# Query and key stacks: one transfer of 48 partitions per half instead of three of 16, the high part stored twice in DRAM

## The reference, cut to what matters

```
q = split_heads(query @ Wq.T + bq)      # 16 heads of 16 features
k = split_heads(key @ Wk.T + bk)
scores = einsum('bhqd,bhkd->bhqk', q, k) / sqrt(16)
scores = where(mask == 0, -1e9, scores)
x = softmax(scores) @ v
```

## Time and profile before

| | |
|---|---|
| runs | 1540.78 us median (1537.13 to 1541.7) |
| the profiled execution | 1551.78 us |
| its span | 1550.0 us |
| granted TensorE clock, mean over the span | 0.915 |
| TensorE matmul busy | 1268.1 us, 82% |
| VectorE busy | 1097.4 us, 71% |
| ScalarE busy | 958.6 us, 62% |
| GpSimd busy | 691.8 us, 45% |
| `ks<-ksplit_d` transfers | 192 of 128 KB |
| `qs<-qsplit_d` transfers | 192 of 128 KB |

### The profile page before, as it was taken

How to read it: one execution, slowest core, us unless ns; L and a number is a source line. 1 busy time by engine, 2 the same in 40 slices (tenths; PEclk the granted TensorE clock), 3 DMA queues, 4 the chain that set the end, 5 groups by cost and what they waited for, 6 DMA issues and landing times.

```text
span 1550.0 us, 29933 instructions
## 1 busy us (share of the span) xinstructions
PE 1268.1 (82%) x9486; PEld 878.3 (57%) x9486; DVE 1097.4 (71%) x3076; ACT 958.6 (62%) x1846; POOL 691.8 (45%) x854
## 2 busy tenths in 40 slices
PE   4962365688899989998999899989998999888875
PEld 4851354456566656665666566656665666555543
DVE  4753342458788878887888788878886777777754
ACT  1220231257777767776777777767766777777774
POOL 2312334235544554456445644565446444444331
PEclk9985586699999989998999999999998999999996
DMA  8772354445445445554544455545444444333200
GB/s 273 228 255 56 99 178 146 142 145 157 142 149 155 152 139 150 152 158 134 151 150 150 151 153 148 154 141 150 142 140 127 132 145 126 120 104 103 76 9 14
DMA packets 169174, 216.84 MB, mean 140 GB/s; under 512 B 19002, under 2 KB 157628, under 8 KB 162492
## 3 DMA queue, kind: packets, MB, share of 16 engines
q1 hardware_dynamic: 162876, 198.15, 41.8%
q0 software_dynamic: 6144, 16.79, 3.2%
HBM read 133.33 MB, written 79.43 MB: 137 GB/s over the span
## 4 chain that ended last, share of the span: by engine, by line
PE 47%; DVE 22%; issue 14%; ACT 5%; DMA 4%; POOL 4%; SPq 3%; DVEq 0%; another core or an unknown queue 0%; POOLq 0%; ACTq 0%
DVE mx L1104 8%; PE mx_pair L1369 5%; PE bank L1330 5%; PE ex_pair L1314 4%; PE bank L1442 4%; PE bank L1340 4%; PE bank L1396 3%; PE mx_pair L1292 3%; PE bank L1390 3%; DVE small L1160 3%; PE mx_pair L1356 3%; PE bank L1450 2%; PE bank L1410 2%; DVE t L1155 2%; DVE bn L899 2%
## 5 line engine op out<-in xcount | busy, mean ns | idle before, releaser
L1104 DVE TENSOR_REDUCE mx<-mx_pair 128x4 f32<-128x1024 f32 x256 | 312.7, 1222 | 60.0 <-PE mx_pair L1369 36.2
L694 POOL TENSOR_TENSOR hid<-hid,t 128x256 f32<-128x256 f32 x256 | 196.3, 771 | 227.4 <-DVE t L1155 226.0
L846 ACT ACTIVATE pt<-ex_pair 128x1024 f32<-128x1024 f32 x256 | 262.1, 1024 | 26.0 <-PE ex_pair L1314 25.8
L1369 PE MATMUL mx_pair<-ks,qs 62*128 62x256 f32 x1024 | 133.3, 336 | 67.8 <-DVE mx L1104 57.8
L1330 PE MATMUL bank<-pt,va 128*32 128x256 f32 x2048 | 169.7, 404 | 2.0 <-ACT ot L852 1.9
L1369 PEld LDWEIGHTS mx_pair<-ks,qs 62*128 62x128 f32 x1024 | 85.6, 196 | 144.0 <-DVE mx L1104 120.1
L871 ACT ACTIVATE hid<-bank 128x256 f32<-128x256 f32 x256 | 98.6, 385 | 109.0 <-PE bank L1340 100.3
L1314 PE MATMUL ex_pair<-qs,ks 64*128 64x256 f32 x1024 | 132.5, 338 | 7.8 <-ACT pt L846 7.7
L1442 PE MATMUL bank<-ew,xst 128*128 x480 | 125.5, 406 | 6.4 <-ACT xst L815 6.2
L1155 DVE SCALAR_TENSOR_TENSOR t<-th,bank 128x256 f32<-128x256 f32 x256 | 106.8, 417 | 33.5 <-ACT th L877 21.2
L661 POOL TENSOR_TENSOR rs<-ve,mhalf 128x2 f32<-128x2 f32 x96 | 68.6, 714 | 132.1 <-DVE ve L905 112.0
(11 more groups left out here) (212 smaller groups left out, 2757.4 us busy)
## 6 DMA issues: line engine op xcount, KB each, us to landing
ks<-ksplit_d SPq DMA_DIRECT2D x192, 128.0 KB
qs<-qsplit_d SPq DMA_DIRECT2D x192, 128.0 KB, 3.1
ys_d<-ys SPq DMA_DIRECT2D x56, 256.0 KB, 2.2
xs<-xs_d SPq DMA_DIRECT2D x24, 512.0 KB
x<-in_x SPq DMA_DIRECT2D x32, 256.0 KB, 3.9
va<-in_ctxT SPq DMA_DIRECT2D x32, 256.0 KB, 3.6
xl<-in_x SPq DMA_DIRECT2D x32, 256.0 KB
x_d<-xl SPq DMA_DIRECT2D x32, 256.0 KB, 3.7
```

Of the source, the lines that this page charges most:

```text
L694: pool.tensor_tensor(part_, part_, t1[:, c % 2], ALU.mult).then_inc(hid_made, 1)
L846: act.activation(pt[:, slot:slot + 2].rearrange("p i a c -> p (i a c)"), ex_pair[:, :], ACT.Exp).then_inc(ex_made[u % 2], 1)
L1104: dve.tensor_reduce(mx[:, t].rearrange("p (r g j) -> p r g j", r=2, j=2)[:, :, g], mx_pair[:, :].rearrange("p (r j s) -> p r j s", r=2, j= ...
L1369: ins = pe.matmul(shared_bank(job, r)[:, j * S:(j + 1) * S], qs[par][rows, 2 * g + j, t * P:(t + 1) * P], ks[par][rows, 2 * g + j, :], sta ...
```

## The change

The DRAM scratch holds three parts of each tensor instead of two, in the order in which the stack wants them. The high part is written twice. A half of a stack is then 48 consecutive partitions, and is filled by one transfer. The counts on the semaphores follow: 48 instead of 32 for written parts, 64 instead of 128 for the k stack, 32 instead of 96 for the q stack. The same number of bytes is read.

```
-        ksplit_d = scratch("ksplit_d", [2, 2, D, S])
-        qsplit_d = scratch("qsplit_d", [2, 2, D, S])
+        ksplit_d = scratch("ksplit_d", [2, ROWS, D, S])
+        qsplit_d = scratch("qsplit_d", [2, ROWS, D, S])
...
                 if job == "k_write":
-                    for i, src in enumerate((ph, pl)):
+                    for i, src in enumerate((ph, ph, pl)):
                         sp.dma_start(ksplit_d[b.par, i].rearrange("(k p) s -> p k s", p=P), src[:].bitcast(F32)).then_inc(k_wr[b.par], 16)
                 if job == "k_read":
-                    landed(sp, k_wr, b, 32)
+                    landed(sp, k_wr, b, 16 * ROWS)
...
-                    for row, i in ((0, 0), (1, 0), (2, 1)):
-                        for r in range(2):
-                            sp.dma_start(ks[b.par][r * HALF + row:r * HALF + row + ROWS * (DH - 1) + 1:ROWS].bitcast(F32),
-                                         ksplit_d[b.par, i].rearrange("(d r h) s -> r d h s", d=DH, r=2)[r]).then_inc(ks_ld[b.par], 16)
+                    for r in range(2):
+                        sp.dma_start(ks[b.par][r * HALF:r * HALF + ROWS * DH].bitcast(F32),
+                                     ksplit_d[b.par].rearrange("c (d r h) s -> r d c h s", d=DH, r=2)[r]).then_inc(ks_ld[b.par], 16)
...
                 if job == "q_write":
-                    for i, src in enumerate((ph, pl)):
+                    for i, src in enumerate((ph, pl, ph)):
                         sp.dma_start(qsplit_d[b.par, i].rearrange("(k p) s -> p k s", p=P), src[:].bitcast(F32)).then_inc(q_wr[b.par], 16)
                 if job == "q_read":
-                    landed(sp, q_wr, b, 32)
+                    landed(sp, q_wr, b, 16 * ROWS)
...
-                    for row, i in ((0, 0), (1, 1), (2, 0)):
-                        for r in range(2):
-                            sp.dma_start(qs[b.par][r * HALF + row:r * HALF + row + ROWS * (DH - 1) + 1:ROWS].bitcast(F32),
-                                         qsplit_d[b.par, i].rearrange("(d r h) s -> r d h s", d=DH, r=2)[r]).then_inc(qs_ld[b.par], 16)
+                    for r in range(2):
+                        sp.dma_start(qs[b.par][r * HALF:r * HALF + ROWS * DH].bitcast(F32),
+                                     qsplit_d[b.par].rearrange("c (d r h) s -> r d c h s", d=DH, r=2)[r]).then_inc(qs_ld[b.par], 16)
```

More of the change, by code:

```diff
@@ L557, in work @@
                     after(sp, kl_made, b)
-                    landed(sp, ks_ld, b.ago(2), 128)
-                    for i, src in enumerate((ph, pl)):
+                    landed(sp, ks_ld, b.ago(2), 64)
+                    for i, src in enumerate((ph, ph, pl)):
                         sp.dma_start(ksplit_d[b.par, i].rearrange("(k p) s -> p k s", p=P), src[:].bitcast(F32)).then_inc(k_wr[b.par], 16)
                 if job == "k_read":
-                    landed(sp, k_wr, b, 32)
+                    landed(sp, k_wr, b, 16 * ROWS)
                     after4(sp, sc_ready[1], b.ago(2), 4)
@@ L575, in work @@
                     after(sp, ql_made, b)
-                    landed(sp, qs_ld, b.ago(2), 96)
-                    for i, src in enumerate((ph, pl)):
+                    landed(sp, qs_ld, b.ago(2), 32)
+                    for i, src in enumerate((ph, pl, ph)):
                         sp.dma_start(qsplit_d[b.par, i].rearrange("(k p) s -> p k s", p=P), src[:].bitcast(F32)).then_inc(q_wr[b.par], 16)
                 if job == "q_read":
-                    landed(sp, q_wr, b, 32)
+                    landed(sp, q_wr, b, 16 * ROWS)
                     after4(sp, sc_ready[1], b.ago(2), 4)
-                    for row, i in ((0, 0), (1, 1), (2, 0)):
-                        for r in range(2):
-                            sp.dma_start(qs[b.par][r * HALF + row:r * HALF + row + ROWS * (DH - 1) + 1:ROWS].bitcast(F32),
-                                         qsplit_d[b.par, i].rearrange("(d r h) s -> r d h s", d=DH, r=2)[r]).then_inc(qs_ld[b.par], 16)
+                    for r in range(2):
+                        sp.dma_start(qs[b.par][r * HALF:r * HALF + ROWS * DH].bitcast(F32),
+                                     qsplit_d[b.par].rearrange("c (d r h) s -> r d c h s", d=DH, r=2)[r]).then_inc(qs_ld[b.par], 16)
                 if job == "max_row":
@@ L699, in work @@
                     after(pool, m01_made, b)
-                    landed(pool, ks_ld, b.ago(2), 128)
+                    landed(pool, ks_ld, b.ago(2), 64)
                     pool.tensor_scalar(mbias[:, b.par], mk[96:98, b.par], 0, nbig[96:98, 0:1], ALU.is_equal, ALU.mult).then_inc(mb_made, 1)
@@ L705, in work @@
                     after(pool, kf_made, b)
-                    landed(pool, q_wr, last_q(b), 32)
+                    landed(pool, q_wr, last_q(b), 16 * ROWS)
                     pool.tensor_tensor(pl[:], pf[:], ph[:].bitcast(F32), ALU.subtract).then_inc(kl_made, 1)
@@ L717, in work @@
                     after(pool, qh_made, b)
-                    landed(pool, k_wr, last_k(b), 32)
+                    landed(pool, k_wr, last_k(b), 16 * ROWS)
                     pool.tensor_tensor(pl[:], pf[:], ph[:].bitcast(F32), ALU.subtract).then_inc(ql_made, 1)
@@ L818, in work @@
                     after(act, kf_made, b)
-                    landed(act, q_wr, last_q(b), 32)
+                    landed(act, q_wr, last_q(b), 16 * ROWS)
                     act.activation(ph[:], pf[:], ACT.Copy).then_inc(kh_made, 1)
@@ L827, in work @@
                     after(act, kl_made, last_k(b))
-                    landed(act, k_wr, last_k(b), 32)
+                    landed(act, k_wr, last_k(b), 16 * ROWS)
                     for dst in (pf, ph):
@@ L1361, in work @@
                     if c == 0:
-                        landed(pe, qs_ld, b, 96)
-                        landed(pe, ks_ld, b, 128)
+                        landed(pe, qs_ld, b, 32)
+                        landed(pe, ks_ld, b, 64)
                     for r in range(2):
```

## The result

The changed kernel takes 1559.38 us (median of four runs, 1554.78 to 1563.3), the kernel before 1541.24 on the same chip (four runs, 1537.13 to 1542.77). The ratio is 1.0112, with a 95% interval of 1.0082 to 1.0142: the change costs 1.1%, about 17 us. 1540 had been predicted, in a range that ended at 1552. The profiled execution took 1563.3 us, with a span of 1561.5 against 1550.0; since the profiled execution of before lay above its timed runs, the two traces are 11.5 us apart where the timed runs are 17 to 18.

What follows compares the result with a forecast made beforehand. TensorE was taken as the bound (busy 82%, 47% of the chain), with SP's issue time mattering only on q's path. For q, +0.8 - 0.8 - 0.3 = -0.3 us, all else 0, gave 1 us less: 1540 us, range 1534 to 1552.

Steps and rivals of the forecast that it cites:

- (a): Third write of q: its transfer queues on the DMA engines and delays q's stack by 0.8 us, bounds +0.47 to +0.9.
- (b): Two reads of the q stack instead of six: first issue to completion 5.4 us instead of 6.2, a shift of -0.8.
- D: In (b), time for 0.79 MB to flow, 2.75 us; as rival, tail clock stays up, about 1534.5 us, chance 0.14.
- (c): q's reads: two issues meet an unusually long issue, up to 1.69 us, less often than six; worth -0.3 us.
- rival B: Long reads flow at a lower rate, TensorE waits 11 us in nine small-margin batches, about 1552 us; chance 0.25.
- x: Shift of the time at which the q stack is complete; forecast -0.3 us, ends near -1.1 and +1.55.
- the margins of the prediction: Time between q stack complete and TensorE's first max product: 0.0 to 1.0 us in nine batches, 1.9 or more in 23.
- (d): SP issues 3.8 us less per batch, but nothing waits for the loads behind q's reads: 0 us.
- (e): k's third write lands 0.8 us later with 4 us of cover, its reads have about 20 us: 0 us.
- (f): Shared buffers stay busy 0.8 us longer; ScalarE's next `q` and `k` come at least 10 us later: 0 us.
- (g): Traffic of 64 more 256 KB transfers, 51 us of DMA time; only q's landing lacks cover, already counted in (a).
- C: Rival: a 48-row transfer uses fewer DMA engines; every batch loses at least 9 us, some 300 us in all; chance 0.03.

Runs made afterwards that it cites:

- three writes and short reads: Kernel before with three writes of each tensor, in q and k, but the six short reads of 16 partitions kept; ratio 1.0063.
- Halves in turn: Kernel before with its six short reads reordered: three rows of the lower half, then three of the upper, instead of alternating; ratio 1.0030.
- neighbours: Kernel before with each of the six short reads filling 16 neighbouring partitions instead of every third one, in both stacks; ratio 1.0082.
- q alone: The change made for the query only, the key left as in the kernel before; ratio 1.0088.
- long reads alone: Kernel before with two writes kept and one read of 48 partitions per half, all rows from the high part, in q and k; ratio 1.0031.
- three writes in k: Kernel before with three writes of k but six reads of 16 partitions of it, q unchanged; ratio 1.0033.
- long reads in k: Kernel before with two writes of k and one 48-partition read per half, all from k's high part, q unchanged; ratio 0.9998.
- third write late: Kernel before with both third writes added, each issued behind its stack's six reads, to scratch that nobody reads; ratio 0.9977.
- the hold: k's writes wait until the same batch's expert gather has landed: with k changed 1.0031, with k's third write 1.0037, in the kernel before 0.9977.
- the unwaited one: Kernel before with a third write of k ahead of the reads, issued last, to scratch nobody reads, the reads not waiting for it; ratio 1.0021.

## Why the prediction was wrong

(a) The third write: the right mechanism, the wrong size. +0.8 had been predicted, with +0.9 as its upper end; it is +1.2 in the median of the batches. In the ordinary batch shown above it is 3.68 less 2.94, 0.74 us, as worked out. The rest comes from batches in which the last write lands late. One of them, in SP's timeline, with the DMA window around it (the row of digits is the engines' busy share in 40 slices of 386 to 391 us):
```profile
385.36 0.37 SPq L577 DMA_DIRECT2D qsplit_d<-ph  x1
...
390.91 1.25 SPq L582 DMA_DIRECT2D qs<-qsplit_d  x2
```
```profile
DMA  0079999999999999989940000000010000000000
...
q8 instruction: 1, 0.02, 1.7%
```
The engines are idle from 388.6, a last short transfer comes near 389.6, and SP goes on at 390.9: 5.55 us from the first write issue, 1.9 more than in the ordinary batch. In that window a fetch of instructions (one packet of 16 KB) runs on the same engines. 9 batches of 32 lie over 1.2 us above the shortest (10 with three writes and short reads), 2 before. Over all batches of the changed kernel the match is close: in 11 such a packet starts within 3.25 us after the first write issue, and they are the 11 slowest, 4.78 to 5.67 us; in the other 21 none does, and they take 3.68 to 4.40. The two slow ones of before have such a packet as well, but other batches there have one and lose little. This is a coincidence in traces; that the fetch is the cause wasn't tested.

(b) The long reads: the step that failed, and by its sign. It said -0.8, with D at 2.75, "from the same reads". From first issue to last landing it is 7.4 us; less the fixed 2.65, D is 4.8, above the upper end of 4.3. With the -0.3 of (c), which is part of the same measured way, -1.1 stood against a measured +0.9. The error was to take the rate of reads that alternate between the halves and skip two of three partitions for a read that does neither. Halves in turn and neighbours show each of the two properties costing by itself. The 0.6 us saved at each of four issues is real (3.70 us of issue became 1.24), but issues were not what set the landing once 128 KB took 0.8 us to move (4.8 over six).
The Trainium skill, "SBUF — State Buffer", section on Door 1 (the DMA port swizzle), which rival B cited, gives an estimate of 4.8 us for D if the fullest port sets it; the landings give 4.8 (7.4 less 2.65), so they agree. That page also spreads 16 neighbouring partitions over fewer ports than 16 that lie three apart, and the landings of 4.3 against 3.1 us agree with it.

(c) Long issues: nothing here contradicts -0.3 (before, the way took 6.5 us in the median where 6.2 had been worked out), but it can't be told apart within +0.9.

Of the rivals B was right, in its place, its sign and its two signs in the profile (7.0 us where 6.5 was the mark, and 16.8 us of idle where 5 was). It was priced at x = +1.55. With the measured +2.0 the margins of the prediction give 1.8 + 1.5 + 1.5 + 1.0 + 2.0 + 1.7 + 1.9 + 1.8 + 2.0 = 15.2 us; q alone cost 0.88%, 13.6 us. The same margins with x = +0.75 (7.25 less 6.5) give 4.2 us for long reads alone, measured 0.31% or 4.8; with the halves in turn 4.2 against 0.30% or 4.7; with neighbours (+1.35) 9.4 against 0.82% or 12.7, in an interval of 7 to 18. So the method of margins held for q, and the prediction failed in the terms of x. That one x of 2.0 for all nine comes so near is luck in part. By each batch's own shift between the two traces the margins give 14.3 us, where TensorE waited 17.1. The nine batches of the list, shifted by 1.5 us in the mean, waited 13.3 (4.6 of it the first batch); seven others, most of them shifted by some 3 us with a late write, waited the other 3.8.

(d) SP's shorter issue was worth nothing, as predicted.

(e) k: the cover of the stack was right, no landing of k is waited for. The cost was not nothing: 0.33%, by the medians all from the third write (three writes in k 1.0033, long reads in k 0.9998). So a zero in (e), (f) or (g) is wrong, and which one stays open. For (f), the shared buffers, the traces show nothing: neither with k alone changed nor with three writes of k does a landing of a written part end a wait of ScalarE or GpSimd. Traffic by itself is cleared (third write late, 0.9977), the gather too (the hold leaves the loss). Whether the wait for the third write or its place in the burst does it, 1.0021 for the unwaited one does not decide.

C is refuted (no batch has 9 us more). D is refuted as well. Between 1300 and 1480 us the waits for q did not vanish, and the granted clock is what it was, 0.95 against 0.94:
```profile
1300.00:1480.00 180.00, 151.39 (x1206) 97.82 (x1204) 135.31 (x307) 127.91 (x232) 72.85 (x88) 0.95 0.47 115
```
DMA is busy 0.47 of that stretch instead of 0.32.

## What to carry to other kernels

A rate measured on short transfers that alternate between partition halves, and leave gaps between partitions, does not hold for one long transfer into a block: before six issues are merged into two, look whether the issues or the transfers set the landing, and try the merged shape alone. Sum such a change as a shift x of one landing and hold it against the margin of every batch, both signs of x; here the margins were right and would have given q's loss. A part that is ready early is best written early: in the changed kernel that gave back 0.65%. In the kernel before, q's high part sent ahead of the low one gained 0.2%, but so did the late third writes, which speed nothing up (0.9977); so that gain isn't shown to come from the early part.

## What the runs showed that was not expected

The shape of a transfer changes what SP pays to issue it. A read of 16 neighbouring partitions takes 420 ns in the median, one of every third partition 589, and one of 48 partitions 607; the shortest issue has the longest landing of the short ones.

The clock at the head of the program differs between executions of one kernel. That with q's high part early was profiled twice, on two chips, in the two runs told above. In the window from 200 to 215 us the granted clock is 0.78 in one and 0.50, the lower of its two levels (1.2 of 2.4 GHz), in the other, and TensorE gets through 51 matmuls in the one and 34 in the other. In the 14 us before it the clock was 0.50 in both, with TensorE busy for 1.0 and 2.1 us. The window and the first `max` products of each, the first run's first:
```profile
200.00:215.00 15.00, 11.89 (x51) 9.54 (x51) 3.95 (x20) 4.42 (x11) 2.16 (x3) 0.78 0.47 148
L1373 PE MATMUL mx_pair<-ks,qs x32: 273/412/577, 274.7 to 292.0; 62*128 62x256 f32 x32
```
```profile
200.00:215.00 15.00, 10.71 (x34) 8.75 (x35) 5.81 (x36) 4.88 (x15) 4.30 (x6) 0.50 0.49 149
L1373 PE MATMUL mx_pair<-ks,qs x28: 276/417/580, 283.0 to 296.1; 62*128 62x256 f32 x28
```
The pipelined stretch starts 8.3 us later (283.0 against 274.7). In three of the twenty profiled executions that window stood at 0.50, in the others between 0.54 and 0.82. 8 us are half of what this change costs (in the changed kernel's own trace, at 0.71 there, the first `max` starts 8.6 us later than before, and 4.6 of that is its wait for q), so two single traces compared by their spans can mislead; ratios over several runs are what decides here.
